# Half of the inner layer's bias added to x by GpSimd, and the last batch's quantised layer done in two halves of its tokens

## The reference, cut to what matters

```python
x = x + 0.5 * _L0_ffn_ref(_layernorm(x), ...)     # gated mixture of low-rank experts
x = x + _L0_attn_ref(_layernorm(x), ...)          # attention in windows of 64
x = x + 0.5 * _L0_ffn_ref(_layernorm(x), ...)
x = x + 0.5 * _L1_ffn_ref(_layernorm(x), weight, bias)
x = x + _L1_attn_ref(_layernorm(x), ...)          # low-rank attention, 8 heads, all 1024 keys
x = x + 0.5 * _L1_ffn_ref(_layernorm(x), weight, bias)
```

```python
scales = max(max(abs(blocks)) / 7.5, eps)
q = nearest_on_grid(blocks / scales)
out = (q * scales) @ wd.T + bias                  # wd: the quantised weight, 128 x 128
```

## Time and profile before

| | before |
|---|---|
| median of 3 runs | 1963.77 us (1962.39 to 1965.16) |
| the profiled execution's own time | 1959.97 us |
| its span in the profile | 1958.2 us |
| PE busy | 1787.4 us, 91% |
| DVE busy | 1365.7 us, 70% |
| ACT busy | 1113.2 us, 57% |
| POOL busy | 1149.6 us, 59% |
| chain that ended last, by engine | PE 65%, DVE 20%, issue 5%, ACT 3%, DMA 2% |

### The profile page before, as it was taken

One profiled execution on the slowest core, in us unless ns is written; L12 is line 12 of the kernel. 1 busy time (PEld: TensorE's weight loads), 2 busy tenths in 40 slices (PEclk: granted clock), 3 DMA queues, 4 the chain that ended last, 5 costly groups with the idle time before them and its releaser, 6 DMA issues.

```text
span 1958.2 us, 40434 instructions
## 1 busy us (share of the span) xinstructions
PE 1787.4 (91%) x15535; PEld 1286.4 (66%) x15535; DVE 1365.7 (70%) x3039; ACT 1113.2 (57%) x2101; POOL 1149.6 (59%) x880
## 2 busy tenths in 40 slices
PE   5589999999559899999999999999999999999994
PEld 4468888887447566666666666666666666666563
DVE  6556666665466777778778778778777777877741
ACT  5356666666345265566566566555665656655551
POOL 4200000000256198898788788788878869877861
PEclk9799999999767799999999999999999999999996
DMA  4666666660000000000001000000001000100000
GB/s 121 146 149 152 147 151 158 154 142 24 25 1 1 1 7 7 10 9 7 10 7 20 7 10 18 9 7 20 7 10 18 9 7 7 21 6 10 18 11 25
DMA packets 198595, 81.55 MB, mean 42 GB/s; under 512 B 152535, under 2 KB 177410, under 8 KB 198274
## 3 DMA queue, kind: packets, MB, share of 16 engines
q1 hardware_dynamic: 198402, 78.97, 18.7%
HBM read 39.83 MB, written 29.88 MB: 36 GB/s over the span
## 4 chain that ended last, share of the span: by engine, by line
PE 65%; DVE 20%; issue 5%; ACT 3%; DMA 2%; SPq 2%; POOL 2%; POOLq 0%; DVEq 0%; ACTq 0%
PE pair L1644 12%; PE pair L1548 9%; DVE amax L1556 8%; PE pair L1603 7%; PE pair L1599 7%; DVE o_inv L1666 4%; PE pair L1655 3%; PE pair L981 2%; DMA keys<-rows_mem 2%; PE pair L962 2%; PE pair L1010 2%; ACT y L521 2%; DVE q_low L1488 2%; PE pair L1383 2%; DVE stats L464 2%
## 5 line engine op out<-in xcount | busy, mean ns | idle before, releaser
L1614 ACT ACTIVATE prob<-pair 128x512 f32<-128x512 f32 x1024 | 603.9, 597 | 481.6 <-PE pair L1603 426.8
L1556 DVE TENSOR_REDUCE amax<-pair 128x1 f32<-128x512 f32 x1024 | 662.7, 675 | 245.2 <-PE pair L1548 243.0
L1548 PE MATMUL pair<-key_hl,q_hi 128*128 128x512 f32 x1024 | 446.6, 439 | 23.2 <-DVE amax L1556 19.2
L1603 PE MATMUL pair<-q_low,key_h 65*128 65x512 f32 x1024 | 406.2, 397 | 0.0
L1599 PE MATMUL pair<-q_hi,key_hl 128*128 128x512 f32 x1024 | 405.3, 396 | 0.4 <-ACT prob L1614 0.4
L1628 POOL TENSOR_TENSOR w_mix<-w_mix,prob 128x1024 f32<-128x1024 f32 x160 | 381.7, 2385 | 27.5 <-ACT prob L1614 10.6
L1628 POOL TENSOR_TENSOR Wm<-Wm,prob 128x1024 f32<-128x1024 f32 x155 | 369.1, 2382 | 29.2 <-ACT prob L1614 13.6
L502 POOL TENSOR_SCALAR veps<-mv 128x8 f32<-128x8 f32 x48 | 11.6, 242 | 523.5 <-DVE mv L472 522.3
L1548 PEld LDWEIGHTS pair<-key_hl,q_hi 128*128 128x128 f32 x1024 | 196.9, 192 | 144.1 <-issue 54.9
L1644 PE MATMUL pair<-prob,values 128*32 128x256 f32 x4096 | 251.7, 387 | 3.4 <-DVE o_norm L1673 3.4
L1082 DVE TENSOR_REDUCE mx_neg<-pair 128x4 f32<-128x512 f32 x256 | 164.8, 686 | 111.8 <-PE pair L1010 111.8
(11 more groups left out here) (189 smaller groups left out, 2393.4 us busy)
## 6 DMA issues: line engine op xcount, KB each, us to landing
rows_mem<-once SPq DMA_DIRECT2D x128, 128.0 KB, 2.0
queries<-rows_mem SPq DMA_DIRECT2D x64, 256.0 KB, 5.0
keys<-rows_mem SPq DMA_DIRECT2D x16, 1024.0 KB, 7.6
rows_mem<-once SPq DMA_DIRECT2D x128, 64.0 KB, 1.9
q_low<-shift_cols SPq DMA_DIRECT2D x512, 0.5 KB, 2.0
yT<-o_norm SPq DMA_DIRECT2D x256, 32.0 KB, 1.8
x<-x_dram SPq DMA_DIRECT2D x8, 512.0 KB, 7.5
out_dram<-x SPq DMA_DIRECT2D x8, 512.0 KB, 3.4
```

Source lines behind the costliest of these rows:

```text
L1548: e.matmul(bank(ROW_BANKS[n % 3]), q_hi[:, k, t * P:(t + 1) * P], key_hl[:, b % 2, i * HALF:(i + 1) * HALF], start=True, stop=True, skip_g ...
L1556: e.tensor_reduce(amax1[:, u % 2, t, i:i + 1], bank(ROW_BANKS[(2 * r + i) % 3]), AX_X, ALU.max).then_inc(*row_maxed.up((r, i)))
L1603: e.matmul(bank(j), key_h1[:, b % 2, ks], q_low[:, k, sl], start=False, stop=True, skip_group_check=True).then_inc(*key_scored.up((g, half)))
L1614: e.activation(prob1[:, g % P_BUFS, half * HALF:(half + 1) * HALF], bank(K_BANKS[(2 * g + half) % 3]), ACT.Exp, scale=SCALE1).then_inc(*ke ...
```

## The change

1. The one-row bias products of this layer (two for each batch, sixteen in all, L1395) are gone. The products now start their banks
2. A tile `half_bias` (128x128: 0.5 * bias in every row) is made once at the start of the low-rank attention: one more one-row product, 128 columns wide, and one VectorE instruction ahead of the copy `bo_all`.
3. GpSimd adds `half_bias` to the batch's x (128x1024) as a fifteenth piece of the table, at r = 48, and VectorE's `x += 0.5 * product` waits for it.
4. For the last batch the pieces go by halves of the tokens (`final`): each piece for half 0, then for half 1. The projection's halves and the layer's four TensorE items of this batch have banks of their own, and the store is two transfers of 256 KB.

The diff, cut:

```diff
-    QUANTISE = dict(zip((20, 21, 22, 24, 26, 27, 28, 29, 30, 31, 32, 33, 36, 41), range(14)))
+    QUANTISE = dict(zip((20, 21, 22, 24, 26, 27, 28, 29, 30, 31, 32, 33, 36, 41, 48), range(15)))
+    FINAL = dict(enumerate(((part, half) for part in range(8) for half in range(2)), start=9))
+    FINAL_BANKS = {("proj", 1): 6, ("quant", 1): 6, ("product", 0): 4, ("product", 1): 5}
...
-    while g < NT * U + 50 or running or waiting:
+    while g < NT * U + 26 or running or waiting:
...
-        if b >= 1 and r in QUANTISE:
+        if b == B and r in FINAL:
+            early.append(((("final", *FINAL[r]), None, None), 1))
+        if 1 <= b < B and r in QUANTISE:
             early.append(((("quantise", b - 1, QUANTISE[r]), None, None), 1))
-        if b >= 1 and r == 48:
+        if b >= 1 and r == (48 if b < B else 24):
             waiting += [(kind, b - 1, i) for kind in ("quant", "product") for i in range(2)]
...
-            run = begin(item, 6 if item[0] in ("proj", "quant", "product") and item[1:] == (B - 1, 1) else 7)
+            run = begin(item, FINAL_BANKS.get((item[0], item[2]), 7) if item[1] == B - 1 else 7)
...
+            elif i == 14:
+                xs = x[:, b * NT:(b + 1) * NT, :]
+                e.wait_ge(*y_ready("d", b))
+                e.tensor_tensor(xs, xs, half_bias[:, :].unsqueeze(1).broadcast_to([P, NT, C]), ALU.add).then_inc(
+                    *half_added.up(b))
...
+        def dve_final(e, part, half):
+
...
+            if part == 0:
+                e.wait_ge(*x_dve.at(("m", b, half)))
+                e.wait_ge(*y_ready(*norm_before("d", b, 4)))
+                for t in range(4 * half, 4 * half + 4):
+                    ins = e.bn_stats(stats[:, k, t, :], x[:, b * NT + t, :])
+                ins.then_inc(*stats_done.up(key))
+                e.wait_ge(*stats_done.at(key))
+                for t in range(4 * half, 4 * half + 4):
+                    ins = e.bn_aggr(mv[:, k, t, :], stats[:, k, t, :])
+                ins.then_inc(*mv_done.up(key))
+            elif part == 3:
+                e.wait_ge(*y_act.at(key))
+                e.wait_ge(*dequant.at(("d", b - 1)))
+                e.tensor_reduce(d_amax[:, cols], y[:, y_at("d", b), ts, :].rearrange("p t (b k) -> p (t b) k", k=QB),
+                                AX_X, ALU.max, apply_absolute_value=True).then_inc(*q_steps.up((key, "amax")))
+                e.wait_ge(*q_steps.at((key, "amax")))
+                e.tensor_scalar(d_scale[:, cols], d_amax[:, cols], FP6_UNIT / 7.5, FP6_UNIT * 1e-30, ALU.mult,
+                                ALU.max).then_inc(*q_steps.up((key, "scale")))
+                e.wait_ge(*q_steps.at((key, "scale")))
+                e.reciprocal(d_rscale[:, cols], d_scale[:, cols]).then_inc(*q_steps.up((key, "recip")))
+
+        def pool_final(e, part, half):
+            b, k = B - 1, norm_at("d", B - 1)
+            ts, cols = final_half(half)
...
+            if part == 1:
+                e.wait_ge(*mv_done.at(key))
+                e.tensor_scalar(veps[:, k, ts], mv[:, k, ts, 1], LN_EPS, None, ALU.add).then_inc(
+                    *mean_done.up((key, 0)))
+                e.wait_ge(*mean_done.at((key, 0)))
+                e.tensor_tensor(rstd[:, k, ts], veps[:, k, ts], halfneg[:, ts], ALU.pow).then_inc(*rstd_done.up(key))
+                e.tensor_scalar(mean_neg[:, k, ts], mv[:, k, ts, 0], -1.0, None, ALU.mult).then_inc(
+                    *mean_done.up((key, 1)))
+                e.wait_ge(*mean_done.at((key, 1)))
+                e.wait_ge(*rstd_done.at(key))
+                e.tensor_tensor(mean_neg[:, k, ts], mean_neg[:, k, ts], rstd[:, k, ts], ALU.mult).then_inc(
+                    *mean_done.up((key, 2)))
+            elif part == 4:
+                e.wait_ge(*xd_turned.at(("d", b - 1, 1)))
+                pool_scale(e, key, y[:, y_at("d", b), ts].rearrange("p t (b k) -> p (t b) k", k=QB), nb // 2,
+                           d_rscale[:, cols], d_tile[:, cols, :])
+            elif part == 6:
+                pool_dequantise(e, key, d_q8[:, cols, :], d_scale[:, cols], d_tile[:, cols, :], nb // 2)
+            elif part == 7:
+                xs = x[:, b * NT + 4 * half:b * NT + 4 * half + 4, :]
+                e.tensor_tensor(xs, xs, half_bias[:, :].unsqueeze(1).broadcast_to([P, 4, C]), ALU.add).then_inc(
+                    *half_added.up((b, half)))
+
...
+            if part == 2:
+                e.wait_ge(*mean_done.at((key, 2)))
+                e.wait_ge(*y_free("d", b))
+                for t in range(4 * half, 4 * half + 4):
+                    ins = e.activation(y[:, y_at("d", b), t, :], x[:, b * NT + t, :], ACT.Identity,
+                                       bias=mean_neg[:, k, t:t + 1], scale=rstd[:, k, t:t + 1])
+                ins.then_inc(*y_act.up(key))
+            elif part == 5:
+                act_round(e, key, d_tile[:, cols, :], d_q8[:, cols, :])
...
-                if a == B - 1 and i == 1:
+                if a == B - 1:
...
             elif kind == "product":
                 e.wait_ge(*xd_copied.at(("d", a, i)))
-                e.matmul(bank(j).rearrange("p (t c) -> p t c", c=C), ones_row[:, :],
-                         b_ffn.unsqueeze(1).broadcast_to([1, NT // 2, C]), start=True, stop=False,
-                         skip_group_check=True)
                 for t in range(NT // 2):
                     c0 = i * HALF + t * P
-                    ins = e.matmul(bank(j)[:, t * C:(t + 1) * C], d_turned[:, c0:c0 + P], wdT, start=False,
+                    ins = e.matmul(bank(j)[:, t * C:(t + 1) * C], d_turned[:, c0:c0 + P], wdT, start=True,
                                    stop=True, skip_group_check=True)
                 ins.then_inc(*products.up(("d", a, i)))
...
                 e.wait_ge(*products.at(("d", a, i)))
+                e.wait_ge(*half_added.at(a if a < B - 1 else (a, i)))
                 e.scalar_tensor_tensor(out=xs, in0=bank(j).rearrange("p (t c) -> p t c", c=C), scalar=0.5, in1=xs,
...
             e.wait_ge(*mla_built.at("row"))
             e.matmul(bank(2)[:, 0:C], ones_row[:, :], bo_row[:, :], start=True, stop=True,
+                     skip_group_check=True)
+            e.matmul(bank(2)[:, C:2 * C], ones_row[:, :], b_ffn, start=True, stop=True,
                      skip_group_check=True).then_inc(*mla_product.up("bo"))
...
             e.wait_ge(*mla_product.at("bo"))
+            e.tensor_scalar(half_bias[:, :], bank(2)[:, C:2 * C], 0.5, None, ALU.mult)
             e.tensor_copy(bo_all[:, :], bank(2)[:, 0:C]).then_inc(*mla_built.up("bo"))
...
-            for b in range(B - 2, B):
-                sync_store(e, b)
-            e.wait_ge(s_out, 16 * B)
+            sync_store(e, B - 2)
+            for half in range(2):
+                e.wait_ge(*x_dve.at(("d", B - 1, half)))
+                ts = slice(half * NT // 2, (half + 1) * NT // 2)
+                e.dma_start(outr[:, B - 1, ts], x[:, (B - 1) * NT + half * NT // 2:(B - 1) * NT + (half + 1) * NT // 2, :]
+                            ).then_inc(s_out, 16)
```

23 lines of the change are left out of this document (21 added, 2 removed).

## The result

The changed kernel takes 1933.84 us (median of 4 runs, 1930.42 to 1942.1), the one before 1963.08 us (1961.69 to 1965.16) on the same chip. The ratio is 0.9856, 95% interval 0.9824 to 0.9889: faster by 29.2 us. 1941.1 was forecast, with a range of 1934 to 1952. The profiled execution took 1933.07 us, its span is 27.1 us shorter than before (1931.1 against 1958.2).

A forecast was written before the change was run, and what follows sets the result against it. TensorE's queue was taken to pace the attention, and a chain of engines taking turns the end. Inside -11.5, setup +0.5 and last batch -11.7 sum to -22.7 us: 1963.8 to 1941.1 us, range 1934 to 1952.

The forecast's parts named there:

- The bias products inside: Fourteen one-row products leave TensorE's queue inside the attention: 11.5 us less, bounds 10.2 and 14.7.
- The first product: First bias product of batches 0 to 5: VectorE had idled 1.33 us, so the full 1.05 us is gained.
- The second: Second bias product of batches 0 to 5: 0.51 of 1.05 us gained, since TensorE then waits for `o_norm`.
- The wait named ahead: Sign in the attention: TensorE waits 0.5 us for `o_norm` behind each second product.
- Batch 6's two: Batch 6's two bias products: VectorE waited 7.92 and 1.66 us for them, so full gain, 2.10 us.
- Rival (a): Inside the attention, VectorE's runs without a pause catch all fourteen products: gain 0 there, 1952.6 us; chance 0.12, large part included.
- rival (e): Nothing changes: the freed time turns up in waits inside the attention and at the end, 1963 us; chance 0.02.
- The additions at nothing: GpSimd's seven additions of 2.38 us before a head's shift fit its idle time: 0 us; 16.7 if uncovered.
- Rival (c): In the attention, GpSimd's additions hold VectorE, each to its end: 16.7 us more, 1957.8 us; chance 0.02.
- Rival (d): GpSimd paces the attention: TensorE's 11.5 us worth nothing, each addition counts in full, 1969.3 us; chance 0.04.
- The setup: Ahead of `bo_all`, one more pair of short TensorE instructions and one VectorE instruction: +0.5 us, bounds 0.3 and 0.9.
- The last batch: At the end: 4.0 us from two bias products, 7.0 from overlapping halves, 0.75 from the last transfer; together 11.7 us.

The follow-up runs named there:

- o_norm_first: The changed kernel with VectorE making `o_norm` ahead of its step's small work, so ahead of the layer's addition: 1932.17 us, 0.9836 of the kernel before.

## Why the prediction was right, and where its sizes were off

The direction, the places and the waits came as forecast. The time lies at the range's fast edge: 1933.84 us against 1934, or, as a share of the kernel before beside it, 0.9856 against 1934 / 1963.8 = 0.985. What was off are three sizes.

**The bias products inside: right, too small.** Forecast 11.5 us, shown 13.2 plus 1.8 from the clock. By its steps for one batch:
- The first product was to give 1.05, since VectorE was not late. It gave about 1.24. Worked out from the starts in TensorE's timeline: a product with a full 128-row operand follows the scores after 0.24 us where the one-row product followed after 0.33, and its own first instruction takes 0.11 us before the next where it took 0.21. The forecast had counted only the one-row product's own 1.05 us and not the starts on either side. VectorE's idle time shows the same: it was to fall from 1.33 to 0.3 us and fell to 0.08. At the second product nothing of this kind is gained: the two starts are 0.47 and 0.21 us with the one-row product and without it, and why the first differs stays open.
- The second was to give 0.51 and lose 0.54 to `o_norm`. It lost 0.43, as o_norm_first shows by giving just that back. The wait named ahead is the wait that came, 0.37 us in each of the six batches.
- Batch 6's two were to give 2.10 in full. The distance 5 to 6, which holds its first, falls by 1.85 like the others. What the six distances don't hold, batch 0's first product and batch 6's second, is 15.0 - 12.8 = 2.2 us: 0.9 ahead of the first, 1.2 between batch 6's two, and 0.1 behind.

Rival (a), that VectorE's queue swallows the gain, held only for 0.43 of the 2.3 us of each batch, and rival (e) for nothing beyond that.

**The additions at nothing: right.** No wait for `half_bias` stands in the trace, the shift still waits for its input, and three times the work costs 2.4 us in one place, which the ratios (0.9856 both) do not show. Rival (c) is out: two further additions beside VectorE's maxima would have cost up to 33 us. VectorE's instructions of L1343's kind are held, but none stands beside an addition. Rival (d) becomes real only with more work than this. The slack was even larger than the 4.43 us read from one row: with three additions the shift of batch 1 starts without a pause behind them, and no batch is longer for it but the last.

**The setup: right.** 0.5 forecast, 0.5 in the trace: `half_bias` takes VectorE's place from 644.21, and `bo_all` starts at 644.4 instead of 643.9. Of this 0.1 comes from ahead; from the one-row product for `bo_all` to `bo_all` itself it is 0.95 us instead of 0.52. Only this short distance shows it, since the start of `bo_all` lies anywhere from 643.4 to 653.1 us in the profiles here.

**The last batch: right, with one term off.** Forecast 11.7 us, shown 12.6. The chain up to the transposes was laid out to 9.2 us and took 9.24. Behind it 6.1 were forecast and 4.75 measured: the products were put at the lower level of the clock, as before, and TensorE's clock came up among them. That 1.3 us was in the text as a bound (2.0) and not in the sum. The transfer gave 0.83 for 0.75. Against them, the projection itself took 0.5 us longer. The last two stretches are luck of the clock in part: in the second profile of the same kernel the products gain only 0.4 us and the projection gives 0.5 instead of taking it, and the end comes out the same.

**The sum.** 22.7 forecast, 27.1 between the spans: 1.7 too little for the bias products inside (about 1.2 of it the starts, 0.5 the shorter wait for `o_norm`), 1.8 from falls of the clock, and 0.9 at the end. The medians differ by another 2.1. Profile and median did not carry over as assumed: runs of one kernel spread over 12 us here (1930.42 to 1942.1). The profiles show one source of it: the attention begins anywhere from 643.4 to 653.1 us, though the work ahead of it is the same in every kernel. What makes that work longer or shorter isn't shown. The two profiles whose attention began at 650 us or later also had more falls of the clock; whether the one brings the other stays open.

## What to carry to other kernels

When an instruction goes from the queue of the bounding engine, look at what each consumer behind it was doing: a consumer that had waited gives the full time, one that had not gives only its own idle time, and the instruction queued behind that one is the next to move (it gave back 0.43 us a batch). Price work given to another engine by the pause at that place and not by the engine's mean load; both VectorE and GpSimd took 2 us pieces for nothing here. When one profile of a tail is compared with another, look at TensorE's level of the clock first: in this one it moved single stretches by 0.8 to 0.9 us with nothing changed. A tail in which the engines take turns is worth splitting in halves even where every piece has a fixed cost, and idle products in the bounding engine's waits there can give back more than they cost.
